# Layers of a fused attention and feed-forward kernel: a root by power on POOL, keys normalised on POOL, transposed queries copied by banks

## The reference

```python
xn = _layernorm(x)
x = x + attn(xn, w_qkv, w_out, b_out, logit_scale) + ffn(xn, Wqkv, q_scale, ..., b2)
```

```python
q, k = l2norm(q) * qs, l2norm(k) * ksc     # t / max(norm(t), 1e-12), per head of 64
q = q * cos * scale + rotate_half(q) * sin * scale
k = k * cos / scale + rotate_half(k) * sin / scale
# windows of 32 tokens look at their own 32 keys and the 32 before
attn = softmax(mask(q @ k.T * 8.0)); out = attn @ v
```

## Time and profile before

| | |
|---|---|
| median of 3 runs | 4268.81 us (4267.52 to 4270.26) |
| the profiled execution | 4268.13 us, of it the span of the trace 4266.1 us |
| attention stage, 0 to 1025 us | PE busy 922.3, DVE 813.9, ACT 577.7, POOL 537.2 us |
| layers, 1025 to 4266 us | PE busy 3030.0, DVE 3079.7, ACT 2026.6, POOL 2138.0 us |
| whole span | PE 93%, DVE 91%, ACT 61%, POOL 63% |

### The profile page before, as it was taken

How to read it: one execution, slowest core, us unless ns; L and a number is a source line. 1 busy time by engine, 2 the same in 40 slices (tenths; PEclk the granted TensorE clock), 3 DMA queues, 4 the chain that set the end, 5 groups by cost and what they waited for, 6 DMA issues and landing times. The chain is left out here.

```text
span 4266.1 us, 124858 instructions
## 1 busy us (share of the span) xinstructions
PE 3952.3 (93%) x48616; PEld 2743.1 (64%) x48616; DVE 3893.6 (91%) x4860; ACT 2604.4 (61%) x3780; POOL 2675.2 (63%) x4692
## 2 busy tenths in 40 slices
PE   7999999996899999999999999999999999999996
PEld 4666666664666666666666666666666666666664
DVE  6888888886999999999999999999999999999994
ACT  4555565563566666666666666666666666666663
POOL 5555555554676766767667676666766767667673
PEclk9999999998999999999999999999999999999999
DMA  5444444441000011000110001100011000010000
GB/s 134 92 92 94 94 94 91 91 93 45 23 16 17 16 30 29 16 17 16 30 29 16 17 16 30 30 16 17 16 29 29 16 17 16 20 38 16 18 15 14
DMA packets 342439, 165.07 MB, mean 39 GB/s; under 512 B 114240, under 2 KB 337472, under 8 KB 341184
## 3 DMA queue, kind: packets, MB, share of 16 engines
q1 hardware_dynamic: 342208, 161.99, 17.1%
HBM read 115.67 MB, written 33.69 MB: 35 GB/s over the span
## 5 line engine op out<-in xcount | busy, mean ns | idle before, releaser
L610 POOL TENSOR_TENSOR pn<-es,rden 128x1024 f32<-128x1024 f32 x192 | 366.3, 1908 | 693.6 <-DVE rden L947 693.6
L706 ACT ACTIVATE y<-ps 128x1024 f32<-128x1024 f32 x384 | 372.2, 1021 | 510.2 <-PE ps L1193 510.2
L614 POOL TENSOR_TENSOR t<-t 128x1024 f32<-128x1024 f32 x192 | 454.3, 2366 | 88.0 <-DVE t L899 88.0
L658 ACT ACTIVATE t<-ps,amx 128x512 f32<-128x512 f32 x512 | 347.6, 688 | 250.9 <-DVE amx L805 250.9
L899 DVE TENSOR_TENSOR t<-ps,tabl 128x512 f32<-128x512 f32 x768 | 490.8, 681 | 0.0
L897 DVE TENSOR_TENSOR t<-ps,tabl 128x1024 f32<-128x1024 f32 x384 | 467.0, 1216 | 16.7 <-ACT sq L722 11.4
L616 POOL TENSOR_TENSOR t<-t 128x1024 f32<-128x1024 f32 x192 | 452.6, 2357 | 3.6 <-DVE t L899 3.6
L1001 DVE TENSOR_TENSOR qn<-t,rn 128x2048 f32<-128x2048 f32 x192 | 438.1, 2282 | 5.1 <-POOL rn L399 5.1
L957 DVE TENSOR_REDUCE ss<-sq 128x32 f32<-128x2048 f32 x192 | 436.9, 2275 | 0.0
L805 DVE TENSOR_REDUCE amx<-ps 128x2 f32<-128x1024 f32 x256 | 310.9, 1215 | 129.5 <-PE ps L1064 129.5
L1042 PEld LDWEIGHTS ps<-cst,qn 128*128 128x128 f32 x3072 | 349.3, 141 | 116.0 <-issue 59.9
(11 more groups left out here) (134 smaller groups left out, 8234.2 us busy)
## 6 DMA issues: line engine op xcount, KB each, us to landing
wm<-values_dram SPq DMA_DIRECT2D x128, 256.0 KB, 5.2
y<-values_dram SPq DMA_DIRECT2D x128, 256.0 KB, 4.9
values_dram<-qT SPq DMA_DIRECT2D x64, 256.0 KB, 2.3
tokens_dram<-x SPq DMA_DIRECT2D x96, 128.0 KB
xs<-tokens_dram SPq DMA_DIRECT2D x192, 64.0 KB, 1.8
xw<-tokens_dram SPq DMA_DIRECT2D x192, 64.0 KB, 1.9
xsh<-x SPq DMA_DIRECT2D x48, 128.0 KB
xsh<-x SPq DMA_DIRECT2D x48, 127.0 KB
```

The costliest lines, as they stand in the source:

```text
L610: nc.gpsimd.tensor_tensor(heads(pn[:], H), heads(es[:], H), rden[:].unsqueeze(2).to_broadcast([P, H, KEYS]), ALU.mult).then_inc(l_p, 1)
L614: nc.gpsimd.tensor_tensor(t1[:, 0:INNER], t1[:, 0:INNER], t2[:, 0:INNER], ALU.add).then_inc(l_rotq, 1)
L706: return act.activation(y[:].rearrange("p h (w q) -> p w h q", w=NW)[:, 2 * half:2 * half + 2], src.rearrange("p (w h q) -> p w h q", w=2, ...
```

## The change

The guess on DVE goes. On POOL a power with exponent -0.5 takes its place, followed by one Newton step: five operations instead of twelve. The factor of the steps is 2 instead of 8192. The multiplication by the root is split: DVE keeps the queries' half, POOL takes the keys' half, with a semaphore `l_kn` of its own. PE signals `l_tq` after each four of the queries' transposes, waits for `l_kn` ahead of the keys' transposes, and ACT copies each bank (128x512) on its own, so that the output product waits for the first copy only, and others for both.

```diff
+        def polish(pool, done, count, root, square, const, tmp):
+            nc.gpsimd.tensor_tensor(root, square, power_const[:, 0:root.shape[-1]], ALU.pow).then_inc(done, 1)
+            pool.wait_ge(done, count * RS_STEP + 1)
+            nc.gpsimd.tensor_tensor(tmp, root, root, ALU.mult).then_inc(done, 1)
+            pool.wait_ge(done, count * RS_STEP + 2)
+            nc.gpsimd.tensor_tensor(tmp, tmp, square, ALU.mult).then_inc(done, 1)
+            pool.wait_ge(done, count * RS_STEP + 3)
+            nc.gpsimd.tensor_tensor(tmp, const, tmp, ALU.subtract).then_inc(done, 1)
+            pool.wait_ge(done, count * RS_STEP + 4)
+            nc.gpsimd.tensor_tensor(root, root, tmp, ALU.mult).then_inc(done, 1)
...
 (POOL)
-                    pool.wait_ge(l_gs, t + 4)
-                    newton(pool, l_rs, t + 3, rn[:], ss[:], rt[:], scaled=True)
+                    pool.wait_ge(l_fl, t + 4)
+                    polish(pool, l_rs, t + 3, rn[:], ss[:], root_const[:], rt[:])
+                if s.has(3):
+                    pool.wait_ge(l_rotk, t + 4)
+                    pool.wait_ge(l_rs, (t + 4) * RS_STEP)
+                    past(pool, l_tk, t + 3)
+                    nc.gpsimd.tensor_tensor(heads(qn[:, INNER:2 * INNER], H), heads(t1[:, INNER:2 * INNER], H),
+                                            rn[:, H:2 * H].unsqueeze(2).to_broadcast([P, H, DH]), ALU.mult).then_inc(l_kn, 1)
...
 (ACT)
-                    act.wait_ge(l_tq, t + 3)
                     past(act, l_s, t + 2)
-                    act.activation(qT[:].rearrange("p h c -> p (h c)"), pool0, ACT.Copy).then_inc(l_qT, 1)
+                    for half in range(2):
+                        act.wait_ge(l_tq, 2 * t + 5 + half)
+                        act.activation(qT[:, 4 * half:4 * half + 4].rearrange("p h c -> p (h c)"), bank(half),
+                                       ACT.Copy).then_inc(l_qT, 1)
...
 (DVE)
                     dve.wait_ge(l_sqk, t + 4)
+                    past(dve, l_kn, t + 3)
                     rotate(1, u, pool1, l_rk)
...
-                    dve.wait_ge(l_fl, t + 4)
-                    nc.vector.tensor_scalar(rn[:].bitcast(I32), ss[:].bitcast(I32), -0.5, float(0x5F3759DF),
-                                            ALU.mult, ALU.add).then_inc(l_gs, 1)
...
-                    dve.wait_ge(l_rs, (t + 4) * RS_POOL)
+                    dve.wait_ge(l_rs, (t + 4) * RS_STEP)
                     dve.wait_ge(l_rotq, t + 4)
-                    dve.wait_ge(l_rotk, t + 4)
-                    past(dve, l_tk, t + 3)
-                    nc.vector.tensor_tensor(heads(qn[:], 2 * H), heads(t1, 2 * H),
-                                            rn[:].unsqueeze(2).to_broadcast([P, 2 * H, DH]), ALU.mult).then_inc(l_qn, 1)
+                    past(dve, l_tq, 2 * t + 6)
+                    nc.vector.tensor_tensor(heads(qn[:, 0:INNER], H), heads(t1[:, 0:INNER], H),
+                                            rn[:, 0:H].unsqueeze(2).to_broadcast([P, H, DH]), ALU.mult).then_inc(l_qn, 1)
...
 (PE)
-                    transposes(0, pool0, qn[:]).then_inc(l_tq, 1)
+                    for half in range(2):
+                        transposes(0, pool0, qn[:], half).then_inc(l_tq, 1)
+                    pe.wait_ge(l_kn, t + 3)
                     past(pe, l_y0sb, t + 1)
                     transposes(1, pool2, qn[:]).then_inc(l_tk, 1)
...
-                        pe.wait_ge(l_qT, t + 3)
+                        pe.wait_ge(l_qT, 2 * t + 5)
```

More of the change, by code:

```diff
@@ L39 @@
 NEG = -1e30
-ROOT_CONSTS = (3.0, 12.0, 768.0)
-ROOT_SCALE = 8192.0
+ROOT_CONST = 3.0
+ROOT_SCALE = 2.0
 RS = 11
 RS_POOL = 12
+RS_STEP = 5
 STEPS = PAIRS * NU
@@ L142, in build @@
         c15 = sb("c15", [P, 2 * H])
-        root_const = sb("root_const", [P, len(ROOT_CONSTS), 2 * H])
+        root_const = sb("root_const", [P, 2 * H])
         floor_const = sb("floor_const", [P, 2 * H])
+        power_const = sb("power_const", [P, 2 * H])
         rn = sb("rn", [P, 2 * H])
@@ L231, in build @@
         l_fl = sem("l_fl")
-        l_gs = sem("l_gs")
         l_rs = sem("l_rs")
@@ L289, in build @@
         l_qn = sem("l_qn")
+        l_kn = sem("l_kn")
         l_tq = sem("l_tq")
@@ L387, in heads, with newton @@
             return ap.rearrange("p (h d) -> p h d", h=n)
-        def newton(pool, done, count, root, half, tmp, steps=range(RS_POOL), scaled=False):
+        def newton(pool, done, count, root, half, tmp, steps=range(RS_POOL)):
             for step in steps:
-                const = root_const[:, step // 4] if scaled else c15[:, 0:root.shape[-1]]
                 to, a, b, op = ((tmp, root, root, ALU.mult), (tmp, tmp, half, ALU.mult),
-                                (tmp, const, tmp, ALU.subtract), (root, root, tmp, ALU.mult))[step % 4]
+                                (tmp, c15[:, 0:root.shape[-1]], tmp, ALU.subtract), (root, root, tmp, ALU.mult))[step % 4]
                 if step:
@@ L554, in _ @@
             nc.gpsimd.memset(c15[:], 1.5).then_inc(s_avg, 1)
-            for k, value in enumerate(ROOT_CONSTS):
-                nc.gpsimd.memset(root_const[:, k], value).then_inc(s_avg, 1)
+            nc.gpsimd.memset(root_const[:], ROOT_CONST).then_inc(s_avg, 1)
             nc.gpsimd.memset(floor_const[:], NORM_FLOOR).then_inc(s_avg, 1)
+            nc.gpsimd.memset(power_const[:], -0.5).then_inc(s_avg, 1)
             nc.gpsimd.memset(ones, 1.0).then_inc(s_avg, 1)
-            pool.wait_ge(s_avg, 3 + len(ROOT_CONSTS))
+            pool.wait_ge(s_avg, 5)
             def copy_batch(b):
@@ L996, in turn @@
                 if s.has(3):
-                    dve.wait_ge(l_rs, (t + 4) * RS_POOL)
+                    dve.wait_ge(l_rs, (t + 4) * RS_STEP)
                     dve.wait_ge(l_rotq, t + 4)
-                    dve.wait_ge(l_rotk, t + 4)
-                    past(dve, l_tk, t + 3)
-                    nc.vector.tensor_tensor(heads(qn[:], 2 * H), heads(t1, 2 * H),
-                                            rn[:].unsqueeze(2).to_broadcast([P, 2 * H, DH]), ALU.mult).then_inc(l_qn, 1)
+                    past(dve, l_tq, 2 * t + 6)
+                    nc.vector.tensor_tensor(heads(qn[:, 0:INNER], H), heads(t1[:, 0:INNER], H),
+                                            rn[:, 0:H].unsqueeze(2).to_broadcast([P, H, DH]), ALU.mult).then_inc(l_qn, 1)
             dve.wait_ge(s_tb, 16)
             scale_tables(0)
-            dve.wait_ge(s_avg, 3 + len(ROOT_CONSTS))
+            dve.wait_ge(s_avg, 5)
             layers(dve, turn)
@@ L1038, in project, with transposes @@
                 return m
-            def transposes(i, pool, src):
-                for a in range(PAIRS):
+            def transposes(i, pool, src, half=None):
+                for a in range(PAIRS) if half is None else range(half * 4, half * 4 + 4):
                     t = nc.tensor.transpose(pool[:, a * P:(a + 1) * P], src[:, i * INNER + a * P:i * INNER + (a + 1) * P], ident)
@@ L1258, in turn @@
                     if s.has(2):
-                        pe.wait_ge(l_qT, t + 3)
+                        pe.wait_ge(l_qT, 2 * t + 6)
                     past(pe, l_xT, t + 4)
```

## The result

The changed kernel takes 4753.42 us (median of 4; 4749.78 to 4756.85) against 4268.17 us (here the median of four runs), ratio 1.1136 with a 95% interval of 1.1117 to 1.1155: 485 us slower, where 4210 us were forecast.

What follows compares the result with a forecast made beforehand. Turn c=0 bound by a ring over four engines, c=1, c=2 and c=3 by PE with its hole. Gains of 0.20, 0.40, 0.31 and 0.31, 1.22 us per batch over 48 batches, give 58.6 us off 4268.1: 4210 us, range 4192 to 4266.

Steps and rivals of the forecast that it cites:

- the price p: Cost of POOL's power, shown in no row: between 0.24 and 3.84 us, taken as 1.0 us.
- The rival "slower": POOL's power costs above 3.1 us, so keys and pn come late; about 4355 us at 3.84, chance 0.13.
- three signs of being wrong: A power above 3 us, pn later than 8.4 us after the windows' product in c=1, or PE idle before keys' transposes.
- the likeliest case: The forecast's own case for the whole kernel: 4195 to 4226 us, chance 0.50.
- Its aside: If POOL wins the race each time, DVE's half ends 8.4 us after the floor and every turn is a microsecond longer.
- The clock is no term of the sum: TensorE's granted clock, 0.9 to 1.0 in every slice after the first, was taken to hold 2.4 GHz throughout.
- PE's hole: PE's 0.33 us wait per turn for ACT's queries copy, between transposes and output product; closing it taken as 0.40 us.
- the ring: Chain from one windows' product through ACT, DVE and POOL to the next; binds c=0, 15.37 us in c=2 and c=3.
- The removal of the guess: DVE's guess after the norm floor, all of it on the ring: 0.20 us, bounds 0.12 and 0.26.
- F+1.40+p: When POOL's root is ready, F being the end of the norm floor; F+4.1 in the kernel before.
- W+6.55+p: When POOL reaches pn after c=0's feed-forward work, W being the windows' product; W+7.9 in the kernel before.
- p of 2.6: In the no-change rival (chance 0.07), DVE ends at F+7.2, 0.2 us late, and c=1 pays 0.80 us: 4267 us.

Runs made afterwards that it cites:

- the cheap power: The changed kernel with the power replaced by a multiplication by 0.01 on the same tiles, so the reciprocal root is left out; 4224.99 us, ratio 0.9891.
- banks and split: The changed kernel without its power: guess and twelve Newton steps kept, multiplication split, queries copied bank by bank; 4317.32 us, ratio 1.0113.
- the copies by banks: The kernel before with one part alone: transposed queries signalled by PE and copied by ACT bank by bank; 4255.05 us, ratio 0.9969.
- the second power: The changed kernel with power and step done first for the queries' 16 columns, then for the keys' (the second power); 4637.83 us, ratio 1.0867.
- the split alone: The kernel before with POOL multiplying the keys and DVE the queries, Newton steps and single copy kept; 4311.01 us, ratio 1.0100.
- banks and no guess: The kernel before with copies by banks and without DVE's guess, the first Newton step starting from a constant tile; 4236.38 us, ratio 0.9926.

## Why the prediction was wrong

**The step that failed is the price p.** "No row shows a power. Below, p is no less than a product of that size, 0.24 us; above I set the whole chain of today, 3.84." The power measured 5.44 us: over five times the 1.0 chosen, and above the upper end. That end was no bound at all, since nothing ties the cost of a power to that of the chain it replaces. The rival "slower" named the right place and its 4355 us was worked out at the false end; its chance of 0.13 was too low for a price that no row bears on. Two of its three signs of being wrong came as named: a power above 3 us, and `pn` in c=1 at W+11.8, later than W+8.4. The third came in another place: PE idles before the queries' transposes, not before the keys'. With the power as cheap as a product the kernel took 4225 us, at the edge of the likeliest case, 4195 to 4226. That it lies inside is in part luck: the turns came down by 1.5 us a batch instead of 1.22, some 15 us more in all, and the fallen clock, which the sum lacks, took about 40 us back (25 turns of 1.66 us, an estimate).

**The order of the halves.** The rival let DVE take its half first. POOL went first, by 0.06 us, in 169 of 192 turns, and DVE's half cost 2.92 us. Its aside, that every turn is then a microsecond longer, is nearly what happened: reversing the order gave back 149 us, 0.8 us a turn.

**The clock.** "The clock is no term of the sum" was true of the kernel before and false of anything that closes PE's hole and leaves c=0 to the ring. (Its "0.9 to 1.0 in every slice after the first" passes over the tenth slice of the earlier trace rows, an 8, where the layers begin.) The hole went to the windows' product at the end of c=0, PE idled 2.1 to 2.4 us there instead of 1.7, and in 15 to 26 of the 48 batches the turn after it lost 1.6 us. In the changed kernel the granted clock of a batch is 0.93. How much of the 485 us that makes was not separated; PE is busy for 157 us more than before (4109.1 against 3952.3) with the same 48616 instructions, and part of that may have fallen where the kernel waits anyway.

**What held.** The ring over four engines, with POOL's additions in it by exclusion; c=0 as bound by the ring, c=1 by PE, c=2 and c=3 by PE with its hole. The forecast 17.1, 16.5, 15.2, 15.2 stands beside 17.10, 16.30, 15.12 and 15.10 with the cheap power. The removal of the guess was under-sized (0.20 for 0.27 in two turns), the hole too (0.40 for 0.57 in c=1). The root at F+1.40+p was exact, and `pn` at W+6.55+p nearly so. That a split with a root so late costs by pn and by DVE's late half was foreseen for p of 2.6, with DVE at F+7.2; with Newton steps DVE ends there too (4311 us).

## What to carry to other kernels

An operation that no row shows has no upper bound in the rows: give its price its own wide spread, and ask at which price the change turns over; here the prediction's sum put that at 2.6 to 3 us. With banks and split and the root at F+4.1, where a power of 2.7 us would put it, the kernel took 4317 us. The guess was still in, but leaving it out was worth only 19 us beside the copies by banks, so the true point lies lower. Where two engines exclude one another and one semaphore releases both, say in code which goes first. Before closing a hole on PE, look where the same idle time will stand next: in these runs the clock stayed while it was spread out, and often fell once it was gathered into one wait.

## What the runs showed of the hardware

A power on POOL costs 5.44 us on 128x32 and 2.92 us on 128x16, about 0.16 us a column, where a product of 128x32 takes 0.25 us.

POOL's power does not hold up a DVE instruction with two SBUF inputs (1.23 us inside a power of 2.90), while POOL's products and DVE's do exclude one another (2.92 for 1.22, 0.85 for 0.22). The Trainium skill, SBUF — State Buffer, section SBUF: two separate sides, says that whichever of the two starts first keeps the shared ports for its whole instruction; the trace agrees for the products and not for the power. By that rule DVE's half would have taken about 4 us beside the second power (an estimate: 2.7 us until the power ends, and its own 1.22).

TensorE's granted clock stayed up behind the 34 waits of 1.6 to 1.8 us at the end of c=0 in the kernel before, and behind 41 such waits with the split alone. Behind waits of 1.9 to 2.6 us at the same place it fell in 15 of 41 cases with the copies by banks, in 21 of 42 with banks and split, in 26 of 37 with banks and no guess, and in 25 of 37 with the cheap power. Why it fell in some and not in others stays open.
